# Opening stage: the first mixed matrix summed by parts of rows ahead of the second quarter, the mixed matrices split in the second pass, zeros first

## The reference

```python
x = L0_attn_x
x = x + 0.5 * _L0_ffn_ref(_layernorm(x), W1, W2, W3)      # silu(x W1') * (x W3'), fwht, W2'
x = x + _L0_attn_ref(_layernorm(x), qkv, o_proj, gamma, beta)
x = x + 0.5 * _L0_ffn_ref(_layernorm(x), W1, W2, W3)
x = x + 0.5 * _L1_ffn_ref(_layernorm(x), gate_w, up_w, down_w, gate_s, up_s, down_s)
x = x + _L1_attn_ref(_layernorm(x), B, C, D)               # tanh(x B') C' + D * x
x = x + 0.5 * _L1_ffn_ref(_layernorm(x), gate_w, up_w, down_w, gate_s, up_s, down_s)
```

## Time and profile before

| | us |
|---|---|
| median of 3 runs | 1722.68 |
| lowest, highest | 1720.81, 2121.18 |
| the profiled execution, its own time | 1721.46 |
| span of its instructions | 1719.7 |
| start of the first matmul | 5.98 |
| start of the first unit | 67.60 |

### The profile page before, as it was taken

The page is one execution under the profiler, slowest core; times in us unless marked ns, Lnnn a source line. Parts: engine busy times, 40 slices in busy tenths (PEclk is TensorE's granted clock), DMA queues, the critical chain, the costliest instruction groups (busy, mean ns, idle before and its releaser), DMA issues. The chain is left out here.

```text
span 1719.7 us, 21358 instructions
## 1 busy us (share of the span) xinstructions
PE 1703.4 (99%) x7696; PEld 1392.2 (81%) x7696; DVE 1155.9 (67%) x1806; ACT 824.0 (48%) x1350; POOL 124.7 (7%) x184
## 2 busy tenths in 40 slices
PE   8999999999999999999999999999999999999998
PEld 6788888888888888888888888888787778787786
DVE  8977678677775555754446554457668869867866
ACT  5745544455675543434223343223556455655534
POOL 1000000000012220000000000000000144100001
PEclk9999999999999999999999999999999999999999
DMA  9775555699985000244345343344556652356665
GB/s 328 265 287 220 220 196 194 238 367 368 371 337 205 1 1 1 107 169 152 136 155 193 136 165 138 148 155 165 220 220 234 234 209 113 140 221 229 237 220 221
DMA packets 76235, 340.33 MB, mean 198 GB/s; under 512 B 7904, under 2 KB 18528, under 8 KB 70496
## 3 DMA queue, kind: packets, MB, share of 16 engines
q1 hardware_dynamic: 76128, 338.93, 52.5%
HBM read 259.73 MB, written 79.17 MB: 197 GB/s over the span
## 5 line engine op out<-in xcount | busy, mean ns | idle before, releaser
L521 PE MATMUL psum<-xc_hi,w 128*128 128x512 f32 x1544 | 609.7, 395 | 1.8 <-DVE xc_lo L1885 1.1
L523 PE MATMUL psum<-xc_lo,w 128*128 128x512 f32 x1544 | 602.2, 390 | 0.0
L525 PE MATMUL psum<-xc_hi,w 128*128 128x512 f32 x928 | 361.3, 389 | 0.0
L521 PEld LDWEIGHTS psum<-xc_hi,w 128*128 128x128 f32 x1544 | 289.8, 188 | 82.6 <-ACT psum L1269 8.1
L521 PE MATMUL psum<-w,hid 128*128 128x512 f32 x864 | 338.0, 391 | 0.7 <-DVE y L1925 0.2
L525 PE MATMUL psum<-w,hid 128*128 128x512 f32 x864 | 336.5, 389 | 0.0
L523 PEld LDWEIGHTS psum<-xc_lo,w 128*128 128x128 f32 x1544 | 290.2, 188 | 56.5
L1918 DVE TENSOR_TENSOR x<-psum,x 128x512 f32<-128x512 f32 x256 | 173.3, 688 | 149.4 <-PE psum L525 149.2
L1942 DVE TENSOR_TENSOR hid<-sg,hid 128x512 fp32r<-128x512 f32 x216 | 150.1, 705 | 92.3 <-ACT hid L1290 90.4
L523 PE MATMUL psum<-w,hid 128*128 128x512 f32 x544 | 211.8, 389 | 0.0
L525 PEld LDWEIGHTS psum<-xc_hi,w 128*128 128x128 f32 x928 | 174.2, 188 | 36.4
(11 more groups left out here) (164 smaller groups left out, 2011.7 us busy)
## 6 DMA issues: line engine op xcount, KB each, us to landing
w<-w_kept SPq DMA_DIRECT2D x186, 896.0 KB, 6.5
w<-w_kept SPq DMA_DIRECT2D x94, 512.0 KB, 7.5
w_kept<-w SPq DMA_DIRECT2D x16, 1792.0 KB, 7.4
w_kept<-prep SPq DMA_DIRECT2D x12, 1792.0 KB, 7.8
w_kept<-w SPq DMA_DIRECT2D x16, 512.0 KB, 6.3
w_kept<-prep SPq DMA_DIRECT2D x12, 512.0 KB, 9.0
att_raw<-in_att_w SPq DMA_DIRECT2D x4, 1024.0 KB, 9.1
x<-in_x SPq DMA_DIRECT2D x4, 1024.0 KB, 12.0
```

The source lines that it names most:

```text
L521: pe.matmul(out, a_hi, b_hi, start=start, stop=False, skip_group_check=onto)
L523: last = pe.matmul(out, a_hi, b_lo, start=False, stop=stop and zero == "a", skip_group_check=onto)
L525: last = pe.matmul(out, a_lo, b_hi, start=False, stop=stop, skip_group_check=onto)
```

## The change

1. The four loads of the first two attention matrices become eight loads of 256 KB by parts of rows, ahead of the second quarter's rows. They are split by parts (`att_part_split`, `att_part_low`), and `mix` runs over the parts j outside and the four banks k inside, in banks 4 to 7. The first mix stands ahead of the second quarter, the second ahead of the third. The quarters 1 and 2 use banks 0 to 3.
2. The mixed matrices are copied as float32 (`mix_copy`, no split) and stored as 1 MB each. In the second pass they are read back by halves, split, and stored again: `mix_raw_load`, `mix_high`, `mix_low`, `mix_split_out`, in and around slots 3, 5, 7 and 9 (`MIX_IN`). All four use one buffer, the region `xn`.
3. TensorE first multiplies zeros (nine matmuls, after a memset by POOL). ScalarE loads its table for Silu at the start.
4. VectorE does slice 7 ahead of low part 6, and sums and split of unit 1 before the first unit; ScalarE likewise. SP's order changes: matrices 2 and 3 ahead of the scratch stores, `scratch_out(2)` behind `w13_out(0)`.
5. POOL does one chunk between the skips of the last tokens of the state space.

The diff, without the lists of semaphores and tiles:

```diff
+            def att_part_raw(j):
+                for i in range(2):
+                    sp.dma_start(att_raw[i][:, j, :], t["att_w"][i][:, j, :]).then_inc(att_part_in[j], 16)
             def att_in_raw(i):
-                sp.dma_start(att_raw[i % 2][:, :, :], t["att_w"][i]).then_inc(att_in[i], 16)
+                sp.dma_start(att_raw[i % 2][:, :, :], t["att_w"][i]).then_inc(att_in[i - 2], 16)
...
             def mix_store(m):
-                sp.wait_ge(mix_ready, KD * (m + 1))
-                sp.dma_start(mix_kept[m], mix_out[m][:, :, :, :].rearrange("p a k d -> p (a k d)").bitcast(F32)
-                             ).then_inc(mix_stored[m], 16)
+                sp.wait_ge(mix_copied, KD * (m + 1))
+                sp.dma_start(mix_raw[m], mix_out[m][:, :, :].rearrange("p k d -> p (k d)")).then_inc(mix_stored[m], 16)
+            def mix_half(r):
+                return slice(r % 2 * 2 * D, (r % 2 + 1) * 2 * D)
+            def mix_raw_load(r):
+                sp.wait_ge(mix_stored[r // 2], 16)
+                if r:
+                    sp.wait_ge(mix_split_kept, 16 * r)
+                else:
+                    sp.wait_ge(xc_ready, conv_base(1) + 7)
+                sp.dma_start(mix_in_raw[:, :, :].rearrange("p k d -> p (k d)"),
+                             mix_raw[r // 2][:, mix_half(r)]).then_inc(mix_raw_in, 16)
+            def mix_split_out(r):
+                sp.wait_ge(mix_ready, r + 1)
+                sp.dma_start(mix_kept[r // 2][:, :, mix_half(r)],
+                             mix_prep[:, :, :, :].rearrange("p a k d -> p a (k d)").bitcast(F32)
+                             ).then_inc(mix_split_kept, 16)
...
                 rows_in(n)
+            for j in range(KD):
+                att_part_raw(j)
             rows_in(4)
-            att_in_raw(0)
             rows_in(5)
-            att_in_raw(1)
             x_load(0)
             x_load(1)
             sp.dma_start(ident[:, :], t["ident"]).then_inc(consts_in, 16)
             flat_load(0)
             sp.wait_ge(fw_ready, 4)
             rows_in(6)
+            for i in range(2):
+                sp.wait_ge(att_lo_done, 2 * KD - 1 + i)
+                att_in_raw(2 + i)
+            scratch_out(0)
             sp.wait_ge(fw_ready, 6)
             rows_in(7)
-            scratch_out(0)
-            for i in range(2):
-                sp.wait_ge(att_lo_done, i + 1)
-                att_in_raw(2 + i)
+            mix_store(0)
             scratch_out(1)
             sp.wait_ge(fw_ready, 7)
             x_load(2)
-            mix_store(0)
-            scratch_out(2)
             sp.wait_ge(fly_ready, len(FW_PARTS))
             flat_load(1)
             mix_store(1)
             w13_out(0)
+            scratch_out(2)
             for j in range(4):
                 sp.wait_ge(scratch_done[j], 48)
             scratch_out(3)
...
+                    if ps.no == 1 and s - 1 in MIX_IN:
+                        mix_split_out(MIX_IN.index(s - 1))
+                        if s - 1 == MIX_IN[-1]:
+                            sp.wait_ge(mix_split_kept, 16 * len(MIX_IN))
+                    if ps.no == 1 and s + 1 in MIX_IN:
+                        mix_raw_load(MIX_IN.index(s + 1))
...
-                        if s >= 2 and i == 0 and not low:
-                            pe.wait_ge(turned, TT * (s - 2) + j + 1)
+                        if s and i == 0 and not low:
+                            if s == 1:
+                                pe.wait_ge(fw_out, j + 1)
+                            else:
+                                pe.wait_ge(turned, TT * (s - 2) + j + 1)
...
-            def mix(m, ks):
-                pe.wait_ge(att_lo_done, 2 * (m + 1))
+            def mix(m, js):
                 a, b = 2 * m, 2 * m + 1
-                for k in ks:
-                    if m:
-                        pe.wait_ge(mix_ready, k + 1)
-                    else:
-                        pe.wait_ge(fw_out, k + 1)
-                    for j in range(KD):
-                        last = three(pe, bank(k), att_hi[a][:, j, k * P:(k + 1) * P],
+                for j in js:
+                    pe.wait_ge(att_lo_done, 2 * KD + 2 if m else 2 * j + 2)
+                    for k in range(KD):
+                        if m and j == 0:
+                            pe.wait_ge(mix_copied, k + 1)
+                        last = three(pe, bank(BV + k), att_hi[a][:, j, k * P:(k + 1) * P],
                                      att_lo[a][:, j, k * P:(k + 1) * P], att_hi[b][:, j, :], att_lo[b][:, j, :],
                                      j == 0, j == KD - 1)
-                    last.then_inc(mix_full, 1)
+                        if j == KD - 1:
+                            last.then_inc(mix_full, 1)
...
+            pe.wait_ge(warm_ready, 1)
+            for _ in range(WARMING):
+                pe.matmul(bank(RING + 2), warm[:, 0:P], warm[:, :], start=True, stop=True)
             pe.wait_ge(had_ready, 2)
             fw_slice(0)
+            mix(0, range(KD))
             fw_slice(1)
-            mix(0, (0, 1, 2))
+            mix(1, (0, 1, 2))
             pe.wait_ge(consts_in, 48)
             start_turns(0)
-            mix(0, (3,))
+            mix(1, (3,))
             fw_slice(2)
-            mix(1, (0, 1))
             start_turns(1)
-            mix(1, (2, 3))
             fw_slice(3)
...
+            def att_part_split(j):
+                act.wait_ge(att_part_in[j], 32)
+                for i in range(2):
+                    copy(att_hi[i][:, j, :], att_raw[i][:, j, :], AF.Copy).then_inc(att_hi_done, 1)
             def att_split(i):
-                act.wait_ge(att_in[i], 16)
+                act.wait_ge(att_in[i - 2], 16)
                 copy(att_hi[i][:, :, :], att_raw[i % 2][:, :, :], AF.Copy).then_inc(att_hi_done, 1)
-            def mix_split(m):
+            def mix_copy(m):
                 act.wait_ge(mix_full, KD * (m + 1))
                 for k in range(KD):
-                    copy(mix_out[m][:, 0, k, :], bank(k), AF.Copy).then_inc(mix_hi_ready, 1)
+                    copy(mix_out[m][:, k, :], bank(BV + k), AF.Copy).then_inc(mix_copied, 1)
+            def mix_high(r):
+                act.wait_ge(mix_raw_in, 16 * (r + 1))
+                copy(mix_prep[:, 0, :, :], mix_in_raw[:, :, :], AF.Copy).then_inc(mix_hi_ready, 1)
...
+                if n == TT:
+                    for j in range(4):
+                        act.wait_ge(scratch_done[j], 32)
...
+            act.wait_ge(pool_step, 1)
+            copy(low_max[:, 1:2], minus_half[:, 0:1], AF.Silu).then_inc(table_in, 1)
             act.wait_ge(had_in, 16)
             copy(had, had_raw[:, :], AF.Copy).then_inc(had_ready, 1)
             copy(neg_had, had_raw[:, :], AF.Copy, scale=-1.0).then_inc(had_ready, 1)
-            for n in range(4):
+            for n in range(3):
                 fw_split(n)
-            att_split(0)
+            att_part_split(0)
+            fw_split(3)
+            for j in range(1, KD):
+                att_part_split(j)
+            for j in range(4):
+                fw_scale(0, j)
             fw_split(4)
             fw_split(5)
-            att_split(1)
-            for s in range(2):
-                for j in range(4):
-                    fw_scale(s, j)
+            att_split(2)
+            att_split(3)
+            mix_copy(0)
+            for j in range(4):
+                fw_scale(1, j)
             for tile in range(TT):
                 normalise(0, tile, xn[:, tile, :]).then_inc(xn_ready, 1)
             fw_split(6)
-            att_split(2)
             for tile in range(TT):
-                turn_out(tile, tile, BV + tile)
-            att_split(3)
-            mix_split(0)
+                turn_out(tile, tile, BX + tile)
+            mix_copy(1)
+            fw_split(7)
+            w13_split(0)
             for tile in range(TT):
                 act.wait_ge(turn_ready, tile + 1)
                 normalise(1, tile, xn[:, tile, :]).then_inc(xn_ready, 1)
+            for tile in range(TT, PT):
+                turn_out(tile, tile, BV + tile - TT)
+            convert(passes[0], 0)
             for j in range(4):
                 fw_scale(2, j)
-            fw_split(7)
-            for tile in range(TT, PT):
-                turn_out(tile, tile, BV + tile - TT)
-            nc.scalar.activation(low_max[:, 1:2], ident[:, 0:1], AF.Silu).then_inc(table_in, 1)
+            w13_split(1)
+            for m in range(1, 4):
+                convert(passes[0], m)
             act.wait_ge(table_in, 1)
-            convert(passes[0], 0)
-            mix_split(1)
-            w13_split(0)
-            convert(passes[0], 1)
-            convert(passes[0], 2)
             fw_scale(3, 0)
...
+            pool.memset(warm[:, :].bitcast(F32), 0.0).then_inc(warm_ready, 1)
...
-            for i in range(TT):
-                state_skip(3, i)
-            for c in range(4):
+            state_skip(3, 0)
+            state_skip(3, 1)
+            chunk()
```

(32 more changed lines are left out.)

## The result

| | before | after |
|---|---|---|
| median of the runs of this comparison, us | 1721.52 | 1753.61 |
| lowest to highest of after, us | | 1751.08 to 1756.84 |
| span of the profiled execution, us | 1719.7 | 1753.1 |

The ratio is 1.0185, with a 95% interval of [1.0174, 1.0196]: the changed kernel is 32 us slower, just inside the 2% and inside the range. One execution of the kernel before took 2121.18 us, and the ratio leaves it out.

The account below looks back on a forecast made before the run. TensorE, busy 99% of the span, was taken to bound the kernel, with second-pass DMA at 0.94. 1721.5 - 0.8 (opening) - 1.0 (state space) + 21.9 (stalls) + 8.8 (clock) = 1750.4, stated as 1750; range 1730 to 1760.

Parts of the forecast that it names:

- Opening: Up to the first unit: new order of loads and engine work gives -0.8 us, ends -3 and +2.
- The signs: Opening: first mix near 15, second near 34.7, first unit at 67 to 68; moving over 3 us means wrong.
- steps 2 and 3: Second pass: four TensorE waits of 4 to 6 us, weights issued behind the mix store; then matmuls 0.427 apart.
- State space: POOL's chunk ahead of two skips starts at 1459.7 instead of 1462.10: -1.0 us, ends 0 and -1.4.
- Stalls: Second pass: late weights cost 5.6 us in slots 4, 6 and 8, 4.4 in 10, 0.7 in 2: 21.9.
- the 5.6: Slot 4: store lands at 390.5, weights at 398.8, TensorE needs them at 393.2, a stall of 5.6 us.
- The odd units: Second pass: the slot after an even one makes up its lag, its weights landing about 0.6 us ahead of need.
- rival (d): Second pass: delays feed each other, odd slots' loads come late too, total 1757 us and more; chance 0.10.
- Clock: After each of four second-pass stalls TensorE runs at 1.2 GHz, 2.2 us each, 8.8 in all.
- Rival (a): Second pass: the same stalls with the clock kept, 1741.6 us; chance 0.22.
- 8.3 against 7.4: Second pass: weights land 8.3 us after the store; the skill page's estimate gives 7.4, the stage 3.6 us less.
- Rival (b): Second pass: SP's wait costs nothing, only traffic counts, 9.7 us, so 1729.4 us; chance 0.05.

Follow-up runs that it names:

- Experiment 6: Changed kernel without any splits, the opening's later matrix loads and second flat load asked for earlier in SP's order: 1717.65 us, ratio 0.9976.
- 5: Kernel before with one edit alone, POOL's chunk between the skips of the last tokens: 1720.83 us, ratio 0.9993.
- experiment 4: Changed kernel plus 20 unused matmuls at the end of the waits ahead of second-pass units 6, 8, 10 and 12: 1748.78 us, ratio 1.0155.
- experiment 2: Kernel of Experiment 1 with raw loads and split stores cut to half their bytes, output not the reference's: 1736.43 us, ratio 1.0077.
- Experiment 1: Changed kernel with the second pass's raw load moved behind the next unit's weights, so SP does not wait ahead of them: 1746.6 us, ratio 1.0141.
- 3: Changed kernel with the splits of the mixed matrices left out, attention reading them unsplit: 1725.29 us, ratio 1.0016.
- second kernel of 9: Changed kernel with mixed matrices stored unsplit and split just ahead of attention, opening transfers in the changed kernel's order: 1725.03 us, ratio 1.0015.
- second kernel of 8: Changed kernel with splits moved to first-pass slots 1, 3, 10 and 12, and the opening's transfers in the new order: 1753.55 us, ratio 1.0186.
- first kernel of 8: Changed kernel with the four splits moved from the second pass to first-pass slots 1, 3, 10 and 12: 1761.22 us, ratio 1.0226.

## Why the prediction was right, step by step

- **Total.** 1750 forecast, 1753.6 measured; in profiled spans +33.4 where the steps gave +28.9. The likeliest case was the one that came. Of the 4.5 us between them 4.3 are the opening's. That the rest came so close is in part luck: the stalls were 0.9 us dearer than forecast, and the clock, 0.7 cheaper, nearly cancels it.
- **Opening: -0.8 forecast, +3.5 measured. The step that failed.** The ends I had for it were -3 and +2, so it came outside them. (The terms written there, +0.2, -0.5 and -0.3, add up to -0.6, not -0.8.) The first mix (15.0) and the first quarter were right. Two terms were wrong. The landing of the transfers was mis-sized: matrix 2 at 28.0 forecast, 29.16 measured, so that the second mix began at 35.96 and not 34.7; the flat matrix at 58.5 forecast, 60.61 measured. The flat matrix comes last and covers the delay of matrix 2: its 2.1 us and 0.4 of VectorE's work behind it are the 2.5 us by which the first unit missed 67.8. And the clock was put at nothing in the opening, though the prediction had it in the second pass: the seven slow matmuls at the head of the first unit cost another 1.5. Experiment 6 shows that the transfers are the cause: with the matrices, the third quarter's rows and the flat matrix earlier in SP's order, the same engine work gives -4.1. The forecast that VectorE's order decides was right only once the transfers were out of its way.
- **The signs.** The first unit was to move by no more than 3 us. Its first matmul moved by 2.7; by the units' starts it is +4.1 at unit 0 and +3.6 at unit 1, so this sign says that the opening's step was wrong. The signs of steps 2 and 3 came as written, except that the profile puts the waits down to "issue" and the landing times have to name the weights.
- **State space: -1.0 forecast, -1.3 measured** (-1.2 by 5 alone); the other 0.2 of the -1.5 lies in the passes around it. In the changed kernel the chunk starts at 1494.46, with the units ahead of it 34.6 us late, so at 1459.9 in old times, where 1459.7 was forecast, and the transposes take 1.91 instead of 2.75.
- **Stalls: 21.9 forecast, 22.8 measured**, by the starts of matmuls: 1.2, 5.0, 6.8, 5.4 and 4.5 at units 4, 6, 8, 10 and 12, against 0.7, 5.6, 5.6, 5.6 and 4.4. The terms of the 5.6: the store landed 2.5 us after the one ahead of it (2.8 forecast, ends 2.1 and 2.8), and the second half of the weights 8.1 after the store (8.3 forecast). Unit 8's 6.8 was not foreseen: from VectorE's split, which frees SP's next round of issues, to the second half of the weights it took 22.9 us (419.19 to 442.07), ahead of unit 6 only 21.1 (381.83 to 402.89). The store and the loads behind it were all slower there; why, no run shows.
- **The odd units** did not stall, as forecast; rival (d) fell.
- **Clock: 8.8 forecast, 8.1 measured** by the spacing of 38 slow matmuls, 6.8 by experiment 4. Rival (a), the clock kept, fell: after waits of 4.5 to 6.8 us TensorE came back at 1.2 GHz, after the one of 1.2 us it did not, nor after those of up to 1.9 in the second pass of experiment 2. The rule of the Trainium skill's "TensorE: Matmul & The Clock Gate", "Part 1: The HAM clock gate", that an idle stretch brings the throttle back, agrees with the rows of the long waits; after waits around 2.5 us the runs show both (below).
- **8.3 against 7.4.** The estimate from "DMA: Bandwidth & Descriptors", "Anatomy of one DMA", in the Trainium skill was 7.4 us for both halves behind the store. The page gives its fit for transfers issued by GpSimd, and here SP issues them, which the prediction doesn't say. The trace has 8.1 ahead of unit 6 and 8.9 ahead of unit 8, so the rows of the kernel before were the better guide.
- **Rival (b) was priced by a fault.** It took 16.0 us of traffic less nine slots' idle time, 9.7 us in all. Experiment 1 is the nearest to that rival made real, and it lost 24.4 us, 15.0 of them in stalls. The idle 0.06 of the slots can't be saved up: SP's store in a slot waits for VectorE's split, and the weights' loads wait until the unit before last is done. Two slots take 29.9 us when nothing stalls; from one stalling unit to the next it was 34.6 to 36.4 us there, by the units' starts. So the traffic of a slot seems to count against that slot's own margin of 0.1 to 1.1 us.

The opening of the same code differs between executions: +3.5 in the changed kernel and in 3, +1.1 in 1, +1.4 in the second kernel of 9. The traces show where. The first matmul of the first unit starts between 69.3 and 70.3 in all of them, and where the opening came out at +3.4 or +3.5 seven or eight matmuls behind it run slow, in the others none. The second kernel of 9 there, to be held against the rows of the changed kernel from 70.32 on:

```profile
69.73 0.47 PE L534 MATMUL psum<-xc_hi,w 128*128 128x512 f32 x1 [2.39 <-DVE xc_lo L1953]
70.04 0.39 PE L536 MATMUL psum<-xc_lo,w 128*128 128x512 f32 x1
```

What stays open is why the clock fell behind some of these waits and not behind others of the same length. With the new order of transfers that wait is 1.2 us, no matmul behind it ran slow, and the opening was -4.1 and -4.2.

## What to carry to other kernels

Transfers added to a stage whose DMA is at 0.94 delayed what is loaded there in both orders tried here; reordering the issues won 7 us of 31, halving the bytes another 12, and taking the split out of the stage nearly all of it. Look for a place where the data are used and the engines stand idle before you send them through memory twice. And an engine with free time in its busy column can still be waiting for one late transfer: print where it waits, since a few loads moved up in SP's list were worth 6 to 8 us here.

## What the runs showed of the hardware

- While SP waited for its own store the DMA engines moved 308 GB/s over 15 us (380 to 395 us); without the wait, in experiment 1, 347, and before the change 362. In the next 15 us it was 349 with the wait and 417, at a share of 1.02, without.
- In the second pass the slow clock came with the longer waits only. Waits of 1.2 to 1.9 us (changed kernel, experiments 1 and 2) and one of 2.2 (experiment 4): none. Two of 2.3 and 2.4 (experiment 1): seven or eight slow matmuls, from the third on. From 3.3 to 6.8 us: seven to thirteen, from the first on. Ahead of the first unit both were seen at almost the same length: none behind 2.4 to 2.65 us in three executions, seven or eight behind 2.5 to 2.7 in four. And at 8 us, in the first quarter, waits of 1.1 to 1.3 were followed by seven slow ones in three executions (2, 3 and the second kernel of 8). All these waits are by the starts of matmuls.
- In experiment 2, where no stall of the second pass was over 1.9 us, the shorter stalls saved 4.0 us and the clock that was kept 8.1.
- From issue to landing 512 KB took 3.2 to 4.5 us right behind a landed store, in the second pass. Behind a store of 1.75 MB in the first pass (first kernel of 8) they took 12.9 in a full stretch and still 9.7 to 10.3 in the others, in a pass where DMA is busy for 0.60 of the time: the share of a stage says little of the wait behind one large transfer.
- Nine matmuls of zeros from 1.33 us on made the first real group of four take 1.17 instead of 2.05, yet the time of the kernel did not change by as much as the runs can tell.
